# 192 channels contracted as 128 and 64 in the state-space networks, the 64-row remainders of two blocks as row tiles in a pair, the bias added by ScalarE

## The reference, cut to what matters

```python
def _mlp(x, w1, b1, w2, b2):
    return jax.nn.silu(x @ w1 + b1) @ w2 + b2
A_log = -jnp.abs(_mlp(x, A_w1, A_b1, A_w2, A_b2))    # 192 -> 384 -> 16
Bv = _mlp(x, B_w1, B_b1, B_w2, B_b2)                 # 192 -> 384 -> 16
Cv = _mlp(x, C_w1, C_b1, C_w2, C_b2)                 # 192 -> 384 -> 16
delta = jax.nn.sigmoid(_mlp(x, d_w1, d_b1, d_w2, d_b2))  # 192 -> 192 -> 192
...
cur = u_t[:, :, None] * dB
state = (dlt[:, :, None] * state + (1.0 - dlt[:, :, None]) * cur) * dA
y = jnp.sum(state * c[:, None, :], axis=2) + u_t * D_param
```

## Time and profile before

| | |
|---|---|
| median of 3 runs | 2004.85 us (1998.23 to 2019.99) |
| profiled execution | 2019.03 us, span of its trace 2017.3 us |
| mean granted TensorE clock | 0.892 of full |
| TensorE busy | 1652.1 us (82%), 11159 matmul instructions |
| VectorE, ScalarE, GpSimd busy | 1073.4, 769.3, 735.4 us |
| the networks of the state-space layer | 1448 to 1570 us of the span |

### The profile page before, as it was taken

One profiled execution on the slowest core, in us unless ns is written; L12 is line 12 of the kernel. 1 busy time (PEld: TensorE's weight loads), 2 busy tenths in 40 slices (PEclk: granted clock), 3 DMA queues, 4 the chain that ended last, 5 costly groups with the idle time before them and its releaser, 6 DMA issues. The chain is left out here.

```text
span 2017.3 us, 34754 instructions
## 1 busy us (share of the span) xinstructions
PE 1652.1 (82%) x11159; PEld 1301.9 (65%) x11160; DVE 1073.4 (53%) x3224; ACT 769.3 (38%) x1401; POOL 735.4 (36%) x680
## 2 busy tenths in 40 slices
PE   3899999959999849877978679999299477756897
PEld 2677777748888736665767679998177233346564
DVE  2688888857777322567175522211520599942332
ACT  0467777714555321452153421111245433324010
POOL 2567667512223114233331103333200299920232
PEclk9999999979999859787977769999599799967999
DMA  3243433222343120000000635553400666544110
GB/s 66 48 94 70 80 77 73 70 79 87 110 110 93 47 64 1 1 2 12 1 2 2 186 105 162 154 159 96 93 1 1 166 158 162 140 110 129 52 48 27
DMA packets 219419, 158.12 MB, mean 78 GB/s; under 512 B 116583, under 2 KB 196405, under 8 KB 218795
## 3 DMA queue, kind: packets, MB, share of 16 engines
q1 hardware_dynamic: 206405, 141.18, 28.4%
q0 software_dynamic: 6528, 14.19, 2.5%
q10 hardware_dynamic: 6374, 1.33, 0.4%
HBM read 106.05 MB, written 32.35 MB: 69 GB/s over the span
## 5 line engine op out<-in xcount | busy, mean ns | idle before, releaser
L2105 POOL TENSOR_TENSOR ssm_scan_prod<-ssm_scan_S,ssm_crep 128x1056 f32<-128x1056 f32 x48 | 159.4, 3321 | 144.8 <-DVE ssm_scan_S L2122 144.8
L1240 PE MATMUL a_psum<-a2w_W,a_hT 128*128 128x256 f32 (+1 forms) x640 | 149.2, 380 | 7.2 <-DVE a_z L1041 6.4
L745 PE MATMUL a_psum<-a_W,a_hT 126*128 126x256 f32 x512 | 134.8, 396 | 0.0
L1240 PEld LDWEIGHTS a_psum<-a2w_W,a_hT 128*128 128x128 f32 (+1 forms) x640 | 118.7, 191 | 22.7 <-issue 8.7
L2146 PE MATMUL ssm_scan_psum<-ssm_ST,ssm_EW 112*128 112x512 f32 (+1 forms) x288 | 103.7, 498 | 23.8 <-PEq L1858 21.2
L2663 PE MATMUL moe_tiles_psum<-moe_tiles_XT,moe_tiles_mine 96*128 96x128 f32 x960 | 118.6, 280 | 2.0 <-DMA moe_tiles_mine<-moe_W 2.0
L2663 PEld LDWEIGHTS moe_tiles_psum<-moe_tiles_XT,moe_tiles_mine 96*128 96x128 f32 x960 | 112.8, 194 | 5.3 <-DMA moe_tiles_mine<-moe_W 2.4
L2122 DVE TENSOR_TENSOR_SCAN ssm_scan_S<-ssm_scan_X,ssm_scan_psum 128x1056 f32<-128x1056 f32 x48 | 113.0, 2353 | 5.0 <-issue 0.9
L745 PEld LDWEIGHTS a_psum<-a_W,a_hT 126*128 126x128 f32 x512 | 90.6, 192 | 30.2 <-issue 21.5
L2146 PEld LDWEIGHTS ssm_scan_psum<-ssm_ST,ssm_EW 112*128 112x128 f32 x288 | 51.5, 192 | 90.6 <-issue 68.6
L540 POOL TENSOR_TENSOR a_rstd<-a_rstd,a_mhalf 128x8 f32<-128x8 f32 x64 | 105.1, 1642 | 5.0
(11 more groups left out here) (635 smaller groups left out, 3950.8 us busy)
## 6 DMA issues: line engine op xcount, KB each, us to landing
ssm_scan_grep<-gains SPq DMA_DIRECT2D x48, 528.0 KB, 4.7
moe_tiles_mine<-moe_W SPq DMA_DIRECT2D x40, 576.0 KB, 3.9
a2w_X<-t SPq DMA_DIRECT2D x192, 96.0 KB
moe_route_raw<-in_L_ffn_w SPq DMA_DIRECT2D x16, 576.0 KB
t<-a_O SPq DMA_DIRECT2D x128, 64.0 KB, 1.8
xrows<-in_x SPq DMA_DIRECT2D x30, 192.0 KB
a_X<-xrows SPq DMA_DIRECT2D x60, 91.9 KB
a_PX<-t SPq DMA_DIRECT2D x96, 48.0 KB
```

The source lines that it names most:

```text
L745: last = nc.tensor.matmul(KQ[q][:, j, :], hT[0:MAIN, q, PARTS * j:PARTS * j + PARTS], W[0:MAIN, :], start=False, stop=True)
L1240: last = nc.tensor.matmul(KQ[:, j, :], hT[i % 2][0:rows, k, PARTS * j:PARTS * j + PARTS], W[0:rows, k, :], start=(k == 0), stop=(k == 4))
L2105: nc.gpsimd.tensor_tensor(prod[n % 2][:], S[n % 2][:], crep[:, cols], ALU.mult).then_inc(s_prod, 1)
```

## The change

`NormedColumns` gets a flag `halves`. Without it (the state-space layer alone), the first half of a round turns channels 0 to 127, 128 columns of weights, and the second turns channels 128 to 191 twice: by a transpose into PSUM rows 0 to 63 and by an ordinary product with the identity into rows 64 to 127. So `xT` holds the last 64 channels twice, in both halves of the partitions. The copies take 128 rows. No ones are written.

`W1` holds rows 0 to 127 and, twice, rows 128 to 191: four DMAs for each network in place of two, with the bias as columns `b1`, 27 DMAs in place of 19. Layer one takes two blocks at a time: both 128-row products, then both 64-row ones, the first block's from partitions 0 to 63, the second's from 64 to 127. The eleventh block of a group goes alone. The wait for a bank stands before the pair. Silu adds the bias. VectorE collects channels 96 to 191 into `xk` by three copies, as L1966 still works on halves of 96.

```diff
--- before.py
+++ after.py
@@ -1734,10 +1734,10 @@
     COPIES = 2 * (NTILE // PER)
     PIECES = [(0, 4), (4, 12), (12, 20)]
 
-    def __init__(self, nc, st, ps, src, rows, xT, ident, xn, affine=None, raw=None, known=None):
+    def __init__(self, nc, st, ps, src, rows, xT, ident, xn, affine=None, raw=None, known=None, halves=True):
         self.nc, self.ps, self.src, self.rows, self.xT, self.ident, self.xn = nc, ps, src, rows, xT, ident, xn
         self.affine, self.raw, self.rounds = affine, raw, 2 if raw is not None else 1
-        self.known = known
+        self.known, self.halves = known, halves
         self.stats = st.sbuf("norm_stats", [TILE, NTILE, 6]) if known is None or raw is not None else None
         self.tmp = st.sbuf("norm_tmp", [TILE, 3, NTILE])
         self.rstd = st.sbuf("norm_rstd", [TILE, NTILE])
@@ -1762,7 +1762,7 @@
     def ones(self, act, other=None):
 
         act.wait_ge(self.consts, 1)
-        for to in (self.xT, other):
+        for to in (self.xT if self.halves else None, other):
             if to is not None:
                 self.nc.scalar.mul(to[HALF:HALF + 1, :, :].rearrange("p a c -> p (a c)"), self.mhalf[HALF:HALF + 1, 0:1].broadcast_to([1, 2 * TOKENS]), -2.0)
 
@@ -1805,7 +1805,13 @@
                 tile = self.PER * g + j
                 pe.wait_ge(self.normed, NTILE * (self.rounds - 1) + tile + 1)
                 c = (1 + n % self.BANKS) * BANK + TILE * j
-                last = self.nc.tensor.transpose(self.ps[0:HALF, c:c + TILE], self.xn[:, tile, HALF * kb:HALF * kb + HALF], self.ident[0:TILE, 0:TILE])
+                if self.halves:
+                    last = self.nc.tensor.transpose(self.ps[0:HALF, c:c + TILE], self.xn[:, tile, HALF * kb:HALF * kb + HALF], self.ident[0:TILE, 0:TILE])
+                elif kb == 0:
+                    last = self.nc.tensor.transpose(self.ps[:, c:c + TILE], self.xn[:, tile, 0:PARTS], self.ident[0:TILE, 0:TILE])
+                else:
+                    self.nc.tensor.transpose(self.ps[0:EMB, c:c + TILE], self.xn[:, tile, PARTS:DIM], self.ident[0:TILE, 0:TILE])
+                    last = self.nc.tensor.matmul(self.ps[EMB:PARTS, c:c + TILE], self.xn[:, tile, PARTS:DIM], self.ident[0:TILE, 0:TILE], start=True, stop=True)
             last.then_inc(self.in_psum, 1)
             if then and kb == 1 and g >= 1:
                 then(g - 1)
@@ -1818,8 +1824,9 @@
         for n in range(self.COPIES):
             g, kb = n // 2, n % 2
             act.wait_ge(self.in_psum, n + 1)
-            out = self.xT[0:HALF, kb, self.PER * TILE * g:self.PER * TILE * (g + 1)]
-            got = self.ps[0:HALF, (1 + n % self.BANKS) * BANK:(1 + n % self.BANKS) * BANK + self.PER * TILE]
+            rows = HALF if self.halves else PARTS
+            out = self.xT[0:rows, kb, self.PER * TILE * g:self.PER * TILE * (g + 1)]
+            got = self.ps[0:rows, (1 + n % self.BANKS) * BANK:(1 + n % self.BANKS) * BANK + self.PER * TILE]
             if self.affine:
                 self.nc.scalar.activation(out, got, ACT.Identity, scale=self.gb[:, 0, kb:kb + 1], bias=self.gb[:, 1, kb:kb + 1]).then_inc(self.turned, 1)
             else:
@@ -1857,8 +1864,10 @@
         s_rep = st.sem("rep")
         with ExitStack() as ctx2:
             s2 = Stage(nc, ctx2, name + "_mlp")
-            xT = s2.sbuf("xT", [HALF + 1, 2, TOKENS])
-            W1 = s2.sbuf("W1", [HALF + 1, 2, 1344])
+            xT = s2.sbuf("xT", [PARTS, 2, TOKENS])
+            xk = s2.sbuf("xk", [HALF, TOKENS])
+            W1 = s2.sbuf("W1", [PARTS, 2, 1344])
+            b1 = s2.sbuf("b1", [PARTS, NL1])
             W2 = s2.sbuf("W2", [PARTS, 3, 3, STATE])
             W2d = s2.sbuf("W2d", [HALF, 2, DIM])
             b2 = s2.sbuf("b2", [PARTS, 1])
@@ -1874,7 +1883,7 @@
             G = s2.sbuf("G", [HALF, 2, COLS])
             xn = s2.sbuf("xn", [TILE, NTILE, DIM])
             ps = s2.psum()
-            norm = NormedColumns(nc, s2, ps, None, rows, xT, ident, xn, known=known)
+            norm = NormedColumns(nc, s2, ps, None, rows, xT, ident, xn, known=known, halves=False)
             s_w, s_l1, s_act, s_l2, s_e2, s_sc, s_dt, s_c, s_edge, s_one, s_dtr, s_sel, s_exp, s_cl, s_ln, s_gain, s_skip = (
                 s2.sem(n) for n in ("w", "l1", "act", "l2", "e2", "sc", "dt", "c", "edge", "one", "dtr", "sel", "exp", "cl", "ln", "gain", "skip"))
             block = ctx2.enter_context(nc.Block())
@@ -1890,10 +1899,14 @@
                 c = 0
                 for m in "ABCd":
                     wide = DIM if m == "d" else 2 * DIM
-                    sp.dma_start(W1[0:HALF, :, c:c + wide], dram(w[m + "_w1"], 0, [(wide, HALF), (HALF * wide, 2), (1, wide)])).then_inc(s_w, 16)
-                    sp.dma_start(W1[HALF:HALF + 1, 1, c:c + wide], dram(w[m + "_b1"], 0, [(wide, 1), (1, wide)])).then_inc(s_w, 16)
+                    sp.dma_start(W1[:, 0, c:c + wide], dram(w[m + "_w1"], 0, [(wide, PARTS), (1, wide)])).then_inc(s_w, 16)
+                    for p0 in (0, EMB):
+                        sp.dma_start(W1[p0:p0 + EMB, 1, c:c + wide], dram(w[m + "_w1"], PARTS * wide, [(wide, EMB), (1, wide)])).then_inc(s_w, 16)
+                    high = HALF if m == "d" else PARTS
+                    first = 3 * "ABCd".index(m)
+                    sp.dma_start(b1[0:high, first:first + wide // high].unsqueeze(2), dram(w[m + "_b1"], 0, [(1, high), (high, wide // high), (1, 1)])).then_inc(s_w, 16)
                     c += wide
-                    n += 2
+                    n += 4
                 for i, (m, slot, _) in enumerate(slots):
                     sp.dma_start(W2[:, i, :, :], dram(w[m + "_w2"], 0, [(STATE, PARTS), (PARTS * STATE, 3), (1, STATE)])).then_inc(s_w, 16)
                     sp.dma_start(b2[32 * slot:32 * slot + STATE, :], dram(w[m + "_b2"], 0, [(1, STATE), (1, 1)])).then_inc(s_w, 16)
@@ -1957,6 +1970,10 @@
                 nc.vector.tensor_tensor(rows[:], rows[:], xn[:], ALU.add).then_inc(s_skip, 1)
 
                 dve.wait_ge(norm.turned, norm.COPIES)
+                nc.vector.tensor_copy(xk[0:32, :], xT[HALF:PARTS, 0, :]).then_inc(s_skip, 1)
+                nc.vector.tensor_copy(xk[32:64, :], xT[0:32, 1, :]).then_inc(s_skip, 1)
+                nc.vector.tensor_copy(xk[64:96, :], xT[32:64, 1, :]).then_inc(s_skip, 1)
+                dve.wait_ge(s_skip, 5)
                 dve.wait_ge(s_edge, 4)
                 dve.wait_ge(s_e2, NB2 * groups)
                 for kb in range(2):
@@ -1964,7 +1981,7 @@
                 for kb in range(2):
                     dve.wait_ge(s_exp, kb + 1)
                     nc.vector.scalar_tensor_tensor(tokens(G[:, kb, :]), ratio[:, kb, :].rearrange("p (i c) -> p i c", c=SEQ), dt[:, kb:kb + 1],
-                                                   xT[0:HALF, kb, :].rearrange("p (i c) -> p i c", c=SEQ), ALU.mult, ALU.mult).then_inc(s_gain, 1)
+                                                   (xk[:] if kb else xT[0:HALF, 0, :]).rearrange("p (i c) -> p i c", c=SEQ), ALU.mult, ALU.mult).then_inc(s_gain, 1)
 
             def l1(ft):
 
@@ -1993,22 +2010,24 @@
                         last.then_inc(s_l2, 1)
 
                 for g in range(groups):
-                    for ft in range(NL1):
-                        c0, rows_ = l1(ft)
-                        n = NL1 * g + ft
-                        wait(pe, s_act, n - 3)
-                        for kb in range(2):
-                            k = HALF + kb
-                            last = nc.tensor.matmul(ps[0:rows_, (n % 4) * BANK:(n % 4) * BANK + GROUP], W1[0:k, kb, c0:c0 + rows_],
-                                                    xT[0:k, kb, GROUP * g:GROUP * g + GROUP], start=(kb == 0), stop=(kb == 1))
-                        last.then_inc(s_l1, 1)
+                    at = slice(GROUP * g, GROUP * g + GROUP)
+                    for ft0 in range(0, NL1, 2):
+                        two = range(ft0, min(ft0 + 2, NL1))
+                        wait(pe, s_act, NL1 * g + two[-1] - 3)
+                        for ft in two:
+                            c0, rows_ = l1(ft)
+                            b = ((NL1 * g + ft) % 4) * BANK
+                            nc.tensor.matmul(ps[0:rows_, b:b + GROUP], W1[:, 0, c0:c0 + rows_], xT[:, 0, at], start=True, stop=False)
+                        for ft in two:
+                            c0, rows_ = l1(ft)
+                            b, p0 = ((NL1 * g + ft) % 4) * BANK, EMB * (ft - ft0)
+                            nc.tensor.matmul(ps[0:rows_, b:b + GROUP], W1[p0:p0 + EMB, 1, c0:c0 + rows_], xT[p0:p0 + EMB, 1, at], start=False, stop=True).then_inc(s_l1, 1)
                     if g >= 1:
                         layer2(g - 1)
                 layer2(groups - 1)
 
             @block.scalar
             def _(act):
-                norm.ones(act)
                 norm.copy(act)
                 act.wait_ge(s_c, 1)
                 nc.scalar.activation(dt[:], ldt[:], ACT.Exp)
@@ -2042,7 +2061,7 @@
                         if g >= 2 and ft == 0:
```

(2 more changed lines are left out.)

## The result

The changed kernel took 2023.83 us (median of 14 runs, 2009.6 to 2029.34) and the kernel before, beside it, 2013.3 us (14 runs, the three of the table above among them): 10.5 us slower. The ratio is 1.0049, 95% interval [1.0029, 1.0069], a small but real loss; the ratios here are estimates over all runs of both kernels and can differ by up to 0.002 from the quotient of the two medians. The forecast was +4 us on the 2004.85 us of those three early runs. The median of before lay between 2011 and 2014 us beside every later kernel too, so about 8 of the 15 us between 2009 and 2023.83 are that base, and about 6.5 are mine. The profiled execution of the changed kernel has a span of 2016.3 us and stands on the lower side of its runs. Its earlier stages, which the change doesn't touch, ran 11.8 us shorter than in the trace of before.

What follows compares the result with a forecast made beforehand. TensorE was taken to bound the stage, as one chain. The later start of layer one (+3.4 us) and its steady part (+0.4) gave +3.8, say +4: 2009 us against the median of 2004.85, range 1996 to 2022.

Steps and rivals of the forecast that it cites:

- the pairs: Layer one, steady: a pair of blocks takes 1.73 us against 1.76; with the eleventh blocks, +0.4 us together.
- what is hidden: Start of layer one: GpSimd's stall absorbs 1.04 us of the later start, copies into xk cost 0; +3.4 us.
- (a): Rival, layer one: the row pair costs no change of shape, -14 us, 1991 us; 7%.
- (c): Rival, layer one: the two 64-row tiles do not overlap, every pair 0.44 us longer, 2026 us; 6%.
- (d): Rival, clock: real products within the turn bring it up before the layers begin, 2006 us; 14%.
- the turn: Turning normalised rows on TensorE before layer one: rounds of 2.48 us, +4.2 us, last copy at about 1464.1.
- I take the first: Choice in the turn: transpose and product share a 64-column shape and run together, +4.2 us, rather than +11.5 in all.
- (b): Rival, the turn: each transpose and product change the shape, +11.5 us more at the front, 2018 to 2021 us; 28%.
- the weights: Weight loads on SP's queue: 27 DMAs add 3.4 to 6 us, complete at 1462.6 to 1465.2, beside the turn.

Runs made afterwards that it cites:

- quads: Changed kernel with layer one's blocks in fours instead of twos, on five banks; VectorE's clamp at 124.21 us from the stage's start against 132.90, one run.
- one-tile kernel: Changed kernel with both 64-row remainders of a pair in the first row tile; VectorE's clamp at 170.26 us from the stage's start against 132.90, one run.
- two products: Changed kernel with the turn's 64-column transpose made a product as well; VectorE's clamp at 126.62 us from the stage's start against 132.90, one run.
- padded ones: Changed kernel with layer one's second product over 128 rows, lower weights zero; VectorE's clamp at 132.38 us from the stage's start against 132.90, one run.

## Why the prediction was wrong where it was

**Right: the pairs.** "1.73 us against 1.76": 1.71 was measured, with the four 64-row passes in the time of two. In and out cost 0.39 us, where L739's rows gave 0.41. The eleventh block took 1.21 where I had about 1.1. A group is 0.10 us shorter instead of 0.05 longer: the sum charged every pair for a way in and out, but a group's first pair takes 0.10 less (1.61), as it follows layer two and not a 64-row pass. From the first product to the clamp the stretch is 1.24 us shorter (108.35 against 109.59): 0.6 us from six groups, 0.65 at the start, where the stall of 1.04 us is gone and the clock rises 5.6 instead of 4.0 us after the first product. The Trainium skill, page "TensorEngine Tiling (Array Packing)", section "Key Properties", has the drain on a change of mode. The pairs and the quads agree with it and show its price here, 0.39 us for the way in and out.

**Right: what is hidden.** Silu with a bias (0.47 us), the copies into xk, GpSimd's stall gone, and of the rivals neither (a) (a pair of 1.3 us) nor (c) (2.1 us, which the one-tile kernel has) held. Nor did (d): at the turn, half of whose passes are now real products, the clock stayed at 0.50.

**Wrong: the turn, "I take the first: the two have the same number of columns".** This step assumed that a transpose and a product overlap, and took that from layer two's column tiles, which are all products. A round is 4.16 us instead of 2.48, and the last copy landed 24.5 us from the start (1460.82) where I had 16.0 (1464.1). Rival (b) held in kind and was priced too high: 0.15 to 0.19 us for each alternation and not 0.2, a round of 4.16 and not 4.8. Its sum also kept the 0.4 us of two shared changes of shape beside the eight single ones. Layer one began 12.8 us later than before; the forecast had 4.6, (b) about 16. With two products the round was 2.48 us: the sum was right for another pair of instructions. The Trainium skill, page "TensorEngine Tiling (Array Packing)", section "Restrictions", says that column tiling disables float32 transposes. By that rule (b) was the likelier, and the trace agrees with it as far as it can: the transpose never ran beside the product. The gaps of 0.75 and 0.89 us above point to the transpose as the one that leaves the shared shape; no run isolates it.

**Wrong in size: the weights.** They came at 18.0 us from the start, where I had 14.5 to 17. A load of 64 rows takes 0.56 us to issue, not "0.3 to 0.4". It cost nothing here, as the turn lasted until 24.5 us, but it became the bound as soon as the turn was mended (18.57).

**The base.** The median of the first three runs of before, 2004.85 us, was below the 2011 to 2014 us that it has had since; that was chance, as the three hold both the lowest (1998.23) and the highest (2019.99) of its 14 runs. The range, drawn about 2004.85, ended 2 us short of the changed kernel's median for both reasons together.

## What to carry to other kernels

Price a pair of tiles by rows of the same kinds of instruction, not of the same shape: a transpose and a product on two column tiles took turns, two products did not. A row tile is paid for per change of shape, so gather the small passes (four blocks here, 8.7 us) before judging it; in twos the price took nearly all of the saving. When the front of a stage is shortened, look for what was hidden behind it (a queue, another engine's memset, a table load), because a stall can be paid twice: the one of 2.64 us here also cost 6.8 us at half clock. Shorter ones behind the rise (1.04 us in the kernel before) left the clock at full.

## What the runs showed that I had not expected

The granted clock rose at very different times. With the 64-row passes one at a time it stayed at half (1.2 GHz) for 48 us after the first product, against 5.6 us with the same passes in pairs and 3.7 with padded ones, with TensorE busy throughout in all three. The 48 us are one run; only the row tile was changed in it, but why the clock stayed down is not shown, and the gap between 5.6 and 3.7 is no wider than the spread among kernels with the same pairs (4.3 to 6.2). During a stall of 2.64 us the clock fell from 2.4 to 1.2 GHz and stayed there for 6.8 us; without the stall it did not fall. A VectorE copy beside a GpSimd memset took 2.96 us instead of 0.43, and 0.43 again once the memset waited for it. And splitting the loads over two queues, with the merged loads, made the weights 3.1 us later (21.6 against 18.5), with issues of up to 3.67 us on the queue that held none of the small columns of b1.
